# Selective-scan layer and feed-forward: the first sequence's rows loaded in four parts, under a plan laid out twice

## The reference

```python
proj = x @ W_in.T;  u, gate = split(proj)                  # 2 x 2048 channels
u = silu(causal_conv4(u) + conv_b)
dt, B, C = split(u @ Wx.T, [64, 80]);  rmsnorm of each
delta = softplus(dt @ Wdt.T + dt_bias)
state = exp(delta * A) * state + (delta * u) * B           # scan over 512 tokens, 2048 channels x 16 states
y = sum_n(state * C) + u * D_param
x = layernorm(x + (y * silu(gate)) @ W_out.T)
x = layernorm(x + x @ W.T + b + lora(x))                   # lora of rank 8, 16, 32 or 64, picked per token
```

## Time and profile before

| | |
|---|---|
| median of 3 runs | 2130.81 us (2130.18 to 2132.18) |
| profiled execution | 2130.14 us, span of its instructions 2127.8 us |
| busy in the span: PE / DVE / ACT / POOL | 2016.5 / 1961.3 / 1478.4 / 1811.4 us |
| DVE scans (L1348) | 1024, 1192.7 us |
| POOL drives (L1824) | 255, 1168.2 us |
| mean granted TensorE clock | 0.992 |
| moved by DMA | 363.21 MB, 171 GB/s over the span |

### The profile page before, as it was taken

One profiled execution on the slowest core, in us unless ns is written; L12 is line 12 of the kernel. 1 busy time (PEld: TensorE's weight loads), 2 busy tenths in 40 slices (PEclk: granted clock), 3 DMA queues, 4 the chain that ended last, 5 costly groups with the idle time before them and its releaser, 6 DMA issues.

```text
span 2127.8 us, 30662 instructions
## 1 busy us (share of the span) xinstructions
PE 2016.5 (95%) x10528; PEld 1523.1 (72%) x10528; DVE 1961.3 (92%) x2376; ACT 1478.4 (69%) x2193; POOL 1811.4 (85%) x776
## 2 busy tenths in 40 slices
PE   8999999999999799999999997999999999899998
PEld 6877778877565477788776555878875557686686
DVE  4469999999999999999999999999999999999944
ACT  5388787887576776777976657676796656957632
POOL 4359998989998999888899998978799998889950
PEclk9999999999999999999999999999999999999999
DMA  8887856554333457655563433575464337454440
GB/s 309 279 279 256 285 190 210 186 180 121 95 116 96 121 168 259 235 186 171 182 189 109 111 97 106 171 278 176 144 202 112 112 94 237 152 167 129 134 145 40
DMA packets 168762, 363.21 MB, mean 171 GB/s; under 512 B 18656, under 2 KB 45408, under 8 KB 168608
## 3 DMA queue, kind: packets, MB, share of 16 engines
q1 hardware_dynamic: 167408, 360.58, 52.8%
q10 hardware_dynamic: 1200, 0.69, 0.1%
HBM read 292.35 MB, written 68.85 MB: 170 GB/s over the span
## 4 chain that ended last, share of the span: by engine, by line
DVE 34%; PE 33%; issue 11%; ACT 4%; POOL 4%; DMA 1%; DVEq 0%; SPq 0%; POOLq 0%; ACTq 0%
DVE drive L1348 19%; DVE y_acc L1373 9%; PE bank L1222 8%; PE state_t L1167 8%; PE bank L1199 4%; PE bank L1201 3%; PE bank L1200 3%; DVE channels L1380 3%; POOL drive L1824 2%; DVE channels L1417 1%; PE bank L1167 1%; ACT decay L1606 1%; DMA w_split<-w_split 1%; POOL y_acc L1829 1%; DVE rows L1427 1%
## 5 line engine op out<-in xcount | busy, mean ns | idle before, releaser
L1824 POOL TENSOR_TENSOR drive<-delta_u,b_bcast 128x2048 f32<-128x2048 f32 x255 | 1168.2, 4583 | 72.0 <-PE state_t L1167 64.1
L1348 DVE TENSOR_TENSOR_SCAN drive<-decay,drive 128x512 f32<-128x512 f32 x1024 | 1192.7, 1204 | 9.0 <-ACT decay L1606 4.6
L1606 ACT ACTIVATE decay<-delta,a_sb 128x512 f32<-128x512 f32 x1024 | 693.6, 688 | 350.5 <-DVE drive L1348 344.7
L1167 PEld LDWEIGHTS state_t<-identity,drive 128*128 128x128 f32 x4096 | 477.6, 141 | 256.8 <-DVE drive L1348 79.0
L1167 PE MATMUL state_t<-identity,drive 128*128 128x128 f32 x4096 | 573.2, 276 | 56.6 <-DVE drive L1348 34.2
L1199 PE MATMUL bank<-cols_high,w_split 128*128 128x512 f32 (+1 forms) x1248 | 528.2, 423 | 29.3 <-DVE cols_low L1492 9.7
L1373 DVE SCALAR_TENSOR_TENSOR y_acc<-state_t,c_rows,y_acc 128x512 f32<-128x512 f32 x699 | 494.5, 732 | 16.6 <-PE state_t L1167 15.1
L1201 PE MATMUL bank<-cols_high,w_split 128*128 128x512 f32 (+1 forms) x1248 | 492.7, 395 | 0.0
L1200 PE MATMUL bank<-cols_low,w_split 128*128 128x512 f32 (+1 forms) x1248 | 490.4, 393 | 0.0
L1222 PE MATMUL bank<-channels,w_raw 128*128 128x512 f32 x896 | 422.8, 593 | 2.0 <-ACT delta L1717 1.5
L1829 POOL TENSOR_TENSOR y_acc<-y_acc,scaled 128x512 f32<-128x512 f32 x261 | 336.1, 1288 | 80.6 <-ACT scaled L1626 80.1
(11 more groups left out here) (215 smaller groups left out, 1421.6 us busy)
## 6 DMA issues: line engine op xcount, KB each, us to landing
w_split<-w_split SPq DMA_DIRECT2D x304, 512.0 KB, 4.2
b_bcast<-b_rows SPq DMA_DIRECT2D x256, 256.0 KB, 3.4
w_raw<-in_w_out SPq DMA_DIRECT2D x112, 256.0 KB, 3.0
w_raw<-in_w_in SPq DMA_DIRECT2D x64, 256.0 KB, 4.1
gates<-scratch SPq DMA_DIRECT2D x64, 256.0 KB, 3.9
scratch<-gates SPq DMA_DIRECT2D x64, 256.0 KB, 4.7
rows<-in_x_rows SPq DMA_DIRECT2D x4, 2048.0 KB, 10.4
out<-rows SPq DMA_DIRECT2D x16, 512.0 KB, 4.3
```

The lines of the kernel that those rows point to most:

```text
L1167: last = engine.transpose(bank[0:tile.shape[1], i * P:(i + 1) * P], tile, identity[:, :])
L1348: engine.tensor_tensor_scan(state, decay[(GT * s + t) % DECAYS][:, :], state, 0.0, ALU.mult, ALU.add).then_inc(signal["scan"])
L1606: engine.activation(decay[i % DECAYS][:, :], delta[:, g % 2, t, :], ACT.Exp, scale=a_sb[:, j, n:n + 1]).then_inc(signal["decay"])
L1824: engine.tensor_tensor(drive[key % DRIVES][:, :, :], du[:, :, :], row, ALU.mult).then_inc(signal["drive"])
```

## The change

`make_plan` now lays the work out twice. The first layout is the old one. In the second, every piece's due time is 0.542 (`PACE`) times the start that the first layout gave it, no shifts are added, and the choice between `add` and `scale`/`sum` is kept as the first made it. Only in the second layout the load of sequence 0's rows is put as four pieces of 512 KB: three `rows_part` and one `rows_load`, each needing the first scan of unit 24, 28, 32 or 36. `SPREAD` and `EARLIER` have no effect. In the emitted program the four transfers wait for no semaphore; only their place in SP's order is set.

```diff
@@ -56,6 +56,13 @@
 ENGINES = ("PE", "DVE", "ACT", "POOL", "SP")
 
 FREE_IN, DUE_EARLIER = 3, 8
+
+PACE, ROWS_BEHIND = 0.542, (24, 28, 32, 36)
+
+SPREAD = 0.0
+
+EARLIER = {
+}
 
 
 def added(s, tt):
@@ -342,7 +349,8 @@
 
     DELAY = {"PE": 0.3, "DVE": 0.14, "ACT": 0.14, "POOL": 0.14, "SP": 2.2}
 
-    def __init__(self):
+    def __init__(self, known=None):
+        self.known = known
         self.pieces, self.work = {}, {e: [] for e in ENGINES}
         self.count, self.total = {}, {}
         self.pools = {"bank": BANKS, "scratch": SCRATCH, "raw": RAW, "split": SPLIT, "dt": 1, "scaled": 1}
@@ -354,12 +362,19 @@
 
 
         assert (stage, key) not in self.pieces, (stage, key)
-        self.pieces[stage, key] = dict(engine=engine, due=due + shift_of(stage, key), us=us, name=(stage, key), needs=list(needs), take=list(take),
+        if self.known is None:
+            due += shift_of(stage, key)
+        elif (stage, key) in self.known:
+            due = PACE * self.known[stage, key] - EARLIER.get(stage, {}).get(key, 0.0)
+        elif stage in ("add", "scale", "sum"):
+            return
+        self.pieces[stage, key] = dict(engine=engine, due=due, us=us, name=(stage, key), needs=list(needs), take=list(take),
                                        give=list(give), spare=spare, kb=kb, order=len(self.pieces), ahead_of=ahead_of)
 
     def either(self, add, scale):
 
-        self.rival[add], self.rival[scale] = (scale, 2), (add, 1)
+        if self.known is None:
+            self.rival[add], self.rival[scale] = (scale, 2), (add, 1)
 
     def done_way(self, names):
 
@@ -376,7 +391,8 @@
             for need in set(piece["needs"]):
                 left[name] += 1
                 for way in [need] if need in self.pieces else need:
-                    then[way].append(name)
+                    if way in self.pieces:
+                        then[way].append(name)
             for what in piece["give"]:
                 to_give[what] = to_give.get(what, 0) + 1
 
@@ -448,8 +464,17 @@
         self.span = now
 
 
+def starts_of(plan):
+
+    return {(stage, key): at for work in plan.work.values() for at, stage, key in work}
+
+
 def make_plan():
-    plan = Plan()
+
+    return lay_out(Plan(starts_of(lay_out(Plan()))))
+
+
+def lay_out(plan):
     put = plan.put
     uses = {}
 
@@ -771,7 +796,12 @@
     put("SP", -188, 1.5, "consts", 0)
     put("ACT", -30, 1.1, "lora_high", 0, [("consts", 0), ("u_mm", (0, DT // 2, 0))])
     put("DVE", -20, 1.1, "lora_rest", 0, [("lora_high", 0)])
-    put("SP", -20, 0.35, "rows_load", 0, [("u_mm", (0, DT - 1, 0))], kb=2048)
+    if plan.known:
+        for tt in range(TT - 1):
+            put("SP", PACE * 180, 0.35, "rows_part", tt, [("scan", (ROWS_BEHIND[tt], 0))], kb=512)
+        put("SP", PACE * 180, 0.35, "rows_load", 0, [("scan", (ROWS_BEHIND[TT - 1], 0))] + [("rows_part", tt) for tt in range(TT - 1)], kb=512)
+    else:
+        put("SP", -20, 0.35, "rows_load", 0, [("u_mm", (0, DT - 1, 0))], kb=2048)
     for b in range(-1, NSEQ):
         beside(b)
     last_rows()
@@ -909,7 +939,7 @@
-        DMAS = ("raw_load", "x_load", "w_load", "w_store", "g_store", "g_load", "rows_load", "rows_store", "b_store", "fetch", "consts", "wf_load", "bias_load")
+        DMAS = ("raw_load", "x_load", "w_load", "w_store", "g_store", "g_load", "rows_load", "rows_part", "rows_store", "b_store", "fetch", "consts", "wf_load", "bias_load")
         signal = {stage: sem(f"{stage}_done") for stage in plan.total if stage not in DMAS}
 
         x_loaded = [sem(f"x_loaded{k}") for k in range(HT)]
@@ -991,7 +1021,7 @@
             elif stage == "fetch":
                 to, by = b_loaded[key % 2], 16
             else:
-                to, by = {"rows_load": rows_loaded, "b_store": b_stored}.get(stage) or out_stored[key[1]], 16
+                to, by = {"rows_load": rows_loaded, "rows_part": rows_loaded, "b_store": b_stored}.get(stage) or out_stored[key[1]], 16
             raised[id(to)] = raised.get(id(to), 0) + by
             landed[stage, key] = (to, raised[id(to)])
 
@@ -1135,10 +1165,12 @@
                     for t in range(GT):
                         e.wait_ge(*done("y_turn", (LAST, NG - 1, t)))
                     engine.dma_start(ffn_bias, ins["ffn_b_row"].partition_broadcast(P)).then_inc(bias_loaded, 16)
+                elif stage == "rows_part" or stage == "rows_load" and key == 0:
+                    tt = key if stage == "rows_part" else TT - 1
+                    engine.dma_start(rows[:, tt, :], x_rows[0, tt * P:(tt + 1) * P, :]).then_inc(rows_loaded, 16)
                 elif stage == "rows_load":
-                    if key:
-                        for tt in range(TT):
-                            e.wait_ge(*done("rows_store", (key - 1, tt)))
+                    for tt in range(TT):
+                        e.wait_ge(*done("rows_store", (key - 1, tt)))
                     engine.dma_start(rows[:, :, :], x_rows[key].rearrange("(a p) h -> p a h", p=P)).then_inc(rows_loaded, 16)
                 elif stage == "rows_store":
                     s, tt = key
```

## The result

| | before | after |
|---|---|---|
| median of the runs | 2130.89 us (16 runs) | 2135.41 us (16 runs, 2132.16 to 2137.59) |
| profiled execution, span of it | 2130.14, 2127.8 us | 2137.59, 2135.2 us |
| mean granted TensorE clock | 0.992 | 0.987 |

The changed kernel takes 1.0019 times as long, 95% interval 1.0012 to 1.0026: 4.0 us more (2.6 to 5.5). The profiled execution is the longest of the 16, so its trace shows somewhat more than the median loses.

The account below looks back on a forecast made before the run. VectorE and GpSimd were taken to have no slack behind the head. Head 0, seam +3.4, third add +0.2 and transfers 0 gave +3.6 us: 2133.7 for the profiled execution, 2134.4 as median; 8-in-10 range 2130.0 to 2137.0.

Parts of the forecast that it names:

- Head: Up to the second softplus: earlier products and copies against new load waits, -0.6 to +1.5 us, taken as 0.
- Its leaving wins nothing by itself: 0: Rows' 2 MB transfer leaving the head: no wait from 96 to 125 us is for a load, so 0.
- Seam: Units 0 to 1: GpSimd's drive holds VectorE's second drive half, so unit 1's scans start 3.44 us later; main term.
- Third add: Add moved ahead of unit 2's scan waits for a transpose behind one more gate product: +0.2 us (0 to 0.5).
- Rival B: Slower than forecast by a late second softplus, a TensorE clock fall near 149 us (1 to 1.7), or both; centre 2136.2, 25%.
- B's own sign: Second softplus later than 136 us or clock under 0.9 in 149 to 153; one gives 2135.4 to 2136.1, both 2137.6.
- B's other part: Head: copies ahead of `u_silu` and `ssm_square` wait for their loads, ending the softplus up to 1.5 us late.
- Does it last?: Behind the seam to the end: later waits move with VectorE's scans and give nothing back; all engines carry +3.6 us.
- A: Seam: the drive does not hold VectorE, or the drive half gets in first, so no seam cost; 2131.2 us, 20%.
- C: A gain: head 0.6 us shorter and GpSimd's drive, 1.1 earlier, sets the pace; -1.7, 2129.1 us, 7%.
- D: Units 24 to 36: the four transfers are not hidden and each holds a weight or fetch; up to +8, 2142.4 us, 3%.

Follow-up runs that it names:

- e2: The kernel before, only the first sequence's rows loaded in four transfers at the changed kernel's places between units 24 and 36: 0.9996 of before, 2132.11 us.
- e3: The changed kernel with the rows in one 2 MB transfer back at the old place in the head: 1.0035 of before, 2139.42 us.
- e1: The changed kernel with VectorE's first drive half and first scan of unit 0 moved back ahead of the second delta*u pair: 1.0000 of before, 2131.02 us.
- e6: The kernel before with only VectorE's order as changed, first drive half and first scan behind the second delta*u pair: 1.0041 of before, 2139.29 us.
- e4: The changed kernel with GpSimd's low half of (19, 1) made ahead of its drive of unit 1: 1.0026 of before, 2135.15 us.
- e5: The changed kernel with thirteen unused fp32 products keeping TensorE busy at about 142 to 148 us: 1.0008 of before, 2133.61 us.
- e7: The changed kernel with VectorE's first drive half and scan moved back and GpSimd's low half (19, 1) ahead of unit 1's drive: 0.9999 of before, 2129.99 us.
- e10: The changed kernel, VectorE's half and scan moved back, GpSimd's low half before its drive, two gate products moved into TensorE gaps: 0.9988 of before, 2129.30 us.
- e7b: Repeat: the changed kernel with VectorE's half and scan moved back and GpSimd's low half ahead of its drive: 0.9992 of before, 2130.11 us.
- e8: The changed kernel with VectorE's half and scan moved back and unit 0's first transposes ahead of a gate product: 0.9998 of before, 2129.94 us.

## Why the prediction was near

*Head, 0 in the sum: mis-sized, it gave 1.36 us* (133.77 against 135.13), outside my -0.6 to +1.5; over three traces of either head, 133.03 to 134.52 against 134.86 to 135.99, the means differ by 1.6. The step that failed is "I take 0, since each gain has a loss of about its size". The gains were larger: the product of delta came 0.83 us earlier (123.25 against 124.08; I had 0.6), and the first softplus came 1.94 us earlier, for which I had 0.4 to 1. It had stood behind a copy that waited 2.00 us for a load; that wait began at 123.44, so that "among the waits from 96 to 125 us none is for a load" misread the rows. The losses that I foresaw came (copy at 110.16 for a load, `u_silu` 0.4 us later, `ssm_square` 1.44), but did not reach the softplus, because TensorE's transposes for delta now stand ahead of those for B; that is read from the rows, no run turned this order back. "Its leaving wins nothing by itself: 0" holds in the old order, as e2 shows; in the new one the room is worth 3.5 us, as e3 shows.

*Seam, +3.44: right.* From the pair to unit 1's first scan it took 13.47 us (147.24 - 133.77) against 10.33 before: +3.14. The half spans 4.38 us and ends 1.1 us behind GpSimd's drive, as said; e1 takes it away, e6 makes it in the old kernel, and in e4 it lasts over a whole drive. The section "Who interferes with whom" of the Trainium skill's SBUF — State Buffer calls the shared port pair an exclusive lock. By that rule, the traces agree, now up to a wait of 4.5 us (e4 and e6).

*Third add, +0.2: right in size.* It waits 0.17 us in every version with the new order.

*Rival B's clock part was no rival but part of the answer.* I priced it at 1 to 1.7 us if it came, with 25% for the whole of B; it came, at the place and by the gap that B names (PE with little to do from 143 to 147). The clock was 0.50 from 148 to 152, which by B's own sign (under 0.9 in 149 to 153) decides for B, and its 2135.4 to 2136.1 holds the measured 2135.41. The sum left this term out, and e5 measures 2.86 us in the trace, 2.3 in time. It was mis-sized because I counted slow transposes alone: six slow products stand between them, and from the first transposes to those that the adds wait for PE took 7.42 us, in e5 4.59 (148.11 to 152.70). B's other part, a late softplus, did not come.

*The sum against the measurement:* -1.4 + 3.1 + 2.9 - 0.1 is +4.5 at unit 2's run (the last term is the rest of the order), where I had +3.6. Two errors, of -1.4 and +2.9, left 1 us: the seam was understood, but that the number came out so near is in part luck. The median's 4.0 to 4.5 agrees with it. The trace's further 2 us (+4.5 at unit 3, +6.5 at the end) are steps at 190, 435 and 630 us, such as e2 and e7 show too where the clock falls, and this execution was the longest of its 16.

*Does it last?* Half right: nothing was given back, but it was not the same shift that was found at the end. DVE's waits for decays of 2.02 us at 186.24 and 0.50 at 190.19 are 1.76 at 190.50 and 1.38 at 195.34, with a clock of 0.72 in 184 to 196 us where it was 0.86; by 204 us the shift has grown by 1.0. *Rivals A, C, D:* fallen, A by the row at 139.58, D by e2 and by the shift, which stays the same over the four transfers. C's head gain was real, but the hold stood behind it; e7 and e10 are C with the hold taken away.

## What to carry over

Where VectorE and GpSimd both multiply SBUF operands, cost each pair of neighbours in the order as whole instructions in turn, and see that a short one on the critical path never asks just behind a long one: here 4.5 us for 1.1 us of work. An engine that idles because of such a hold can cost as much again in its clock, so cost the work behind a new gap on TensorE at half speed, all of it, not only what is waited for. And a transfer that nobody waits for in the old order may still be what the new order needs gone.

## What was new of the hardware

- A VectorE product of 1.1 us that asks at the same time as a GpSimd product (recorded 0.06 and 0.07 us behind it, e4 and e6) waited for the whole of its 4.6 us, both times.
- TensorE's clock falls in a busy kernel behind gaps of 1.2 to 1.8 us, or doesn't, with the same instructions and gaps: at 435 and 630 us it fell in seven of the twelve traces (the changed kernel, e2, e3, e4, e7, e7b, e8) and stayed full in before, e1, e5 and e6, as in e10 with its moved products. A fall cost the scans 0.7 to 1.2 us there, 1.6 in e6 and 2.3 in e10 at 1040 to 1060, 2.9 at the seam. Such steps make up much of the difference between these traces, in either direction, and they ate e7's 2.3 us. What decides is open. That work in the gap keeps the clock is supported at the seam, where it fell in all four traces with the hold and an idle TensorE (the changed kernel, e3, e4, e6) and not in e5; by e10 it is not shown.
